# Running the query projection of a graph attention layer inside the stage before it

## The reference, cut to what matters

```python
x = _layernorm(x + _L2_gnn_ref(x, ...), axis=-1)       # third layer; its end is "L2b" and the norm "self"
...
q = linear(x, wq, bq)
k = linear(x, wk, bk)
scores = jnp.sum(q[dst] * k[src], axis=-1) * scale
...
out = jax.ops.segment_sum(v[src] * attn[:, None], dst, num_segments=n)
x = layer_norm(x + out + linear(x, ws, bs), g1, b1)
```

## Time and profile before

| what | value |
|---|---|
| median of 3 runs | 3149.26 us (3144.26 to 3154.49) |
| profiled execution: its span, which is also all that the page gives of its own time | 3626.7 us |
| busy in the profile: PE, PEld | 2379.2 us (66%), 1641.7 us (45%) |
| busy: DVE, ACT, POOL | 1987.0 us (55%), 1393.1 us (38%), 2230.6 us (62%) |
| chain that ended last: PE, issue, DVE, unknown | 39%, 21%, 15%, 14% |
| mean granted TensorE clock | 0.711 |

### The profile page before, as it was taken

The page is one execution under the profiler, slowest core; times in us unless marked ns, Lnnn a source line. Parts: engine busy times, 40 slices in busy tenths (PEclk is TensorE's granted clock), DMA queues, the critical chain, the costliest instruction groups (busy, mean ns, idle before and its releaser), DMA issues.

```text
span 3626.7 us, 45558 instructions
## 1 busy us (share of the span) xinstructions
PE 2379.2 (66%) x9551; PEld 1641.7 (45%) x9551; DVE 1987.0 (55%) x7379; ACT 1393.1 (38%) x3670; POOL 2230.6 (62%) x2460
## 2 busy tenths in 40 slices
PE   5655556838777774667777624554556588888888
PEld 2323334724444442344444424444454356555567
DVE  4554446536666673566666813333345366666677
ACT  2444544413333343333333513333343244444444
POOL 5666663566676657666766356666644366666636
PEclk7677677955666677666666755555555789999999
DMA  6656654234444423344444122222212255555411
GB/s 198 176 173 169 172 173 135 63 107 113 114 115 115 114 68 101 108 114 114 116 115 113 26 44 45 47 47 45 47 36 74 74 154 154 155 155 154 148 53 49
DMA packets 247934, 389.14 MB, mean 107 GB/s; under 512 B 58944, under 2 KB 161366, under 8 KB 247673
## 3 DMA queue, kind: packets, MB, share of 16 engines
q0 software_dynamic: 92032, 230.64, 24.6%
q1 hardware_dynamic: 155641, 155.59, 14.0%
HBM read 331.11 MB, written 54.91 MB: 106 GB/s over the span
## 4 chain that ended last, share of the span: by engine, by line
PE 39%; issue 21%; DVE 15%; another core or an unknown queue 14%; POOL 4%; ACT 3%; DVEq 2%; DMA 1%; SPq 0%; POOLq 0%; ACTq 0%
PE PS L1798 20%; PE PS L1719 6%; PE PS L1690 4%; DVE ACC L1323 3%; PE PS L1852 3%; POOL work L690 2%; DVE ACC L1090 1%; DVE work L1294 1%; PE PS L1776 1%; POOL rstd L579 1%; DVEq L376 1%; PE PS L1835 1%; PE PS L1748 1%; PE PS L1769 1%
## 5 line engine op out<-in xcount | busy, mean ns | idle before, releaser
L690 POOL DMA_INDIRECT work<-t_z,srcK x1248 | 1228.2, 984 | 610.8 <-issue 302.5
L1798 PE MATMUL PS<-work,M 128*128 128x260 f32 (+3 forms) x3328 | 1303.0, 512 | 447.6 <-issue 229.0
L1798 PEld LDWEIGHTS PS<-work,M 128*128 128x128 f32 x3328 | 757.4, 270 | 672.1 <-issue 480.2
L1323 DVE TENSOR_TENSOR ACC<-ACC,PS 128x260 f32 (+3 forms) x1614 | 588.7, 365 | 212.7 <-PE PS L1798 117.6
L2026 ACT ACTIVATE M<-iota,dloc 128x128 f32<-128x128 f32 x1248 | 396.9, 389 | 665.3 <-PE PS L1798 308.4
L690 POOL DMA_INDIRECT work<-t_x,srcK x416 | 394.0, 947 | 269.5 <-PE PS L1798 142.2
L690 POOL DMA_INDIRECT work<-in_x,srcTile x392 | 374.8, 956 | 212.2 <-issue 103.7
L1690 PE MATMUL PS<-work,M 128*128 x832 | 313.0, 519 | 240.8 <-issue 120.0
L1690 PEld LDWEIGHTS PS<-work,M 128*128 128x128 f32 x832 | 187.5, 250 | 361.5 <-issue 338.6
L1294 DVE TENSOR_TENSOR work<-work 128x256 f32<-128x256 f32 x800 | 329.1, 412 | 22.4 <-issue 14.2
L1719 PE MATMUL PS<-Y,w 128*128 x832 | 282.3, 425 | 72.2 <-issue 34.8
(11 more groups left out here) (266 smaller groups left out, 2928.9 us busy)
## 6 DMA issues: line engine op xcount, KB each, us to landing
work<-t_dhot SPq DMA_DIRECT2D x416, 128.0 KB
t_hot<-M SPq DMA_DIRECT2D x104, 256.0 KB
M<-t_hot SPq DMA_DIRECT2D x104, 256.0 KB
work<-t_z,srcK POOLq DMA_INDIRECT x1248
t_dhot<-work SPq DMA_DIRECT2D x104, 128.0 KB
work<-t_edge SPq DMA_DIRECT2D x104, 64.0 KB
work<-t_x,srcK POOLq DMA_INDIRECT x416
t_z<-Y SPq DMA_DIRECT2D x50, 130.0 KB, 2.0
```

The costliest lines, as they stand in the source:

```text
L690: pool.indirect_dma_start(out=slots[:, j, 0:width], out_offset=None, in_=table[:, :], in_offset=bass.IndirectOffsetOnAxis(ap=sources[:, k: ...
L1323: ins = vec.tensor_tensor(sums, sums, PS[k % SUMS[stage]][:, 0:cols], ALU.add)
L1798: mm(PS[k % n][:, 0:cols], M[:, k % (4 * G), :], slots_of[:, k % RING[stage], 0:cols], start=True, stop=True)\
```

## The change

The stage Q is dissolved. On PE, ACT and DVE a new helper `beside` takes one slot of the second part of L2b's dense stage and then one slot of the query work, and at the end finishes what is left of the queries. The lags of the query work are 2 (turn), 4 (product), 3 (copy) and 7 (put). It has semaphores of its own (`kept_turned`, `kept_copied`). POOL and SP are untouched. PE waits for the last sum of the pass before the second part, since the queries use the four banks of the sums. The clearing of `ACC` now stands behind all of `put_query`.

```diff
+def beside(main, other):
+    for _ in main:
+        next(other, None)
+    finish(other)
...
-        TURNS = ["L0", "L1", "L2a", "L2b", "Q", "T", "L3"]
+        TURNS = ["L0", "L1", "L2a", "L2b", "T", "L3"]
...
+        kept_turned = signal("kept_turned", {"Q": BLOCKS})
+        kept_copied = signal("kept_copied", {"Q": BLOCKS})
...
-            def gat_edges(stage, hops):
+            def gat_edges(stage, hops, other=()):
...
-                if stage == "L3":
-                    flow([(0, put_query)])
...
-                    finish(slots(EARLY, BLOCKS, hops))
+                    beside(slots(EARLY, BLOCKS, hops), iter(other))
...
-                              (7, free_variance("self", kept, "L2b")), (6, mean_variance("self"))])
+                              (7, free_variance("self", kept, "L2b")), (6, mean_variance("self"))],
+                      slots(0, BLOCKS, [(7, put_query)]))
...
-            def gat_edges(stage, hops, behind=0):
+            def gat_edges(stage, hops, behind=0, other=()):
...
-                    finish(slots(EARLY, BLOCKS, hops))
+                    if other:
+                        pe.wait_ge(sum_added.sem, sum_added.at(stage, STEPS))
+                    beside(slots(EARLY, BLOCKS, hops), iter(other))
...
-            gat_edges("L2b", [(0, turned_block("L2b", ACC, loop_added, 1, HID)), (2, self_branch)], 4)
-            flow([(0, turned_block("Q", X, kept)), (1, queries)])
+            gat_edges("L2b", [(0, turned_block("L2b", ACC, loop_added, 1, HID)), (2, self_branch)], 4,
+                      slots(0, BLOCKS, [(2, turned_block("Q", X, kept, signal=kept_turned, copied=kept_copied)), (4, queries)]))
...
-            finish(slots(EARLY, BLOCKS, outs))
-            flow([(0, turned_copy("Q", xT))])
+            beside(slots(EARLY, BLOCKS, outs), slots(0, BLOCKS, [(3, turned_copy("Q", xT))]))
```

More of the change, by code:

```diff
@@ L1841, in turned_input, with turned_block @@
                 return turned(layer, lambda b, v: rows[:, INPUT + v, 0:D], input_ready, in_turned, in_copied, 0, chunks)
-            def turned_block(layer, tile, ready, chunks=KC, width=D):
-                return turned(layer, lambda b, v: at_block(tile, b)[:, 0:width], ready, in_turned, in_copied, None, chunks)
+            def turned_block(layer, tile, ready, chunks=KC, width=D, signal=in_turned, copied=in_copied):
+                return turned(layer, lambda b, v: at_block(tile, b)[:, 0:width], ready, signal, copied, None, chunks)
             def turned_middle(layer):
@@ L1927, in queries @@
             def queries(b, v, r):
-                pe.wait_ge(in_copied.sem, in_copied.at("Q", b + 1))
+                pe.wait_ge(kept_copied.sem, kept_copied.at("Q", b + 1))
                 if due(b - 1):
@@ L2097, in work @@
                 def work(b, v, r):
-                    act.wait_ge(in_turned.sem, in_turned.at(layer, b + 1))
+                    act.wait_ge(kept_turned.sem, kept_turned.at(layer, b + 1))
                     if due(b - 1):
@@ L2101, in work @@
                     sc.activation(o[:, b % 2, :, :], turn_bank(layer, b)[:, 0:D].rearrange("p (k n) -> p k n", k=KC), ACT.Copy)\
-                        .then_inc(in_copied.sem, 1)
+                        .then_inc(kept_copied.sem, 1)
                 return work
```

## The result

| | median of the runs | ratio to before |
|---|---|---|
| before | 3149.08 us (3140.82 to 3154.50, 20 runs) | |
| changed | 3157.05 us (3149.41 to 3160.39, 20 runs) | 1.0023, 95% interval 1.0017 to 1.0029 |

The kernel became slower by 5 to 9 us, which is within the 0.3% that was called no change. The profiled execution of the changed kernel is an ordinary one: its span is 3147.5 us and its own time 3149.41. The forecast of 3593 us for the profiled execution failed, because what had lengthened the profiled execution of before by 477 us did not come back. So a new profile of the unchanged kernel is needed as the other side of the comparison.

What follows compares the result with a forecast made beforehand. The prediction took POOL's stream of gathers to bound the kernel. Start 2, middle 0, drain 2 and tail 3 delay L3's gathers by 7 us; less 1 for gather 48 gives +6 us, 3155 us, range 3128 to 3170.

Steps and rivals of the forecast that it cites:

- start: DVE's slot 7 of L2b's second part ends with put 0, which waits for PE's product 0: +2.0 us.
- middle: DVE's 2.17 us slots: a put of 0.43 us fits into the 0.65 us wait for POOL: 0 us.
- drain: DVE's slots where blocks only leave have no wait, so six puts cost at most 2.6 us; taken as +2.0.
- tail: End of the dense stage: puts between DVE's last shifts +1.0, ACT's last applied behind a query copy +2.0; together +3.0 us.
- gather 48: L3's gather that waits for the first summed step; the change saves its wait, 0 to 3 us, taken as -1.
- Stage Q is already hidden, by a hair: Before L3: step 0 would release gather 48 at 2842.2, and by its own pace it is due at 2842.3.
- PE at 2.4 GHz from about 2757: Mixed slots: PE works without a gap from slot 2, so its slot takes 1.65 us, faster than DVE's 2.17.
- rival B: PE stays at 1.2 GHz in the mixed part: last block 28 us late, 3177 us; chance 0.17 with partial forms.
- In the runs about 3 us are left for all waits of all gathers together: All passes: 2056 gathers at 1.252 us plus 571.7 us give 3146.5 us; the runs need 3149.26.
- A: The profiled 50.89 us wait in L3 exists in the runs: 34 us back, 3115 us; chance 0.19 with partial forms.
- C: L3 is bound by PE, not by gathers, so the earlier first summed step counts: -7 us, 3142; chance 0.12.
- D: The queries aren't ready when L3 could start, so it starts as before; needs PE at 1.2 GHz; no chance given.

Runs made afterwards that it cites:

- e0: The kernel before, unchanged, run and profiled a second time: 3143.37 us, ratio 1.0005 to before.
- e3: The changed kernel with the lag of put_query 8 in place of 7, so that put 0 doesn't wait: 3145.70 us, ratio 1.0013 to before.
- e4: The changed kernel with query work only in the first 15 slots of DVE and 14 of PE and ACT, the rest afterwards: 3149.94 us, ratio 1.0009.
- e7: The changed kernel with query work in the first slots only and POOL's scale_outs ahead of all power: 3148.07 us, ratio 1.0005 to before.
- e6: The changed kernel with POOL's 15 scale_outs ahead of all power: 3151.56 us, ratio 1.0011 to before.
- e1: The kernel before with the query projection left out altogether: 3143.31 us, ratio 1.0008 to before.
- e2: The kernel before with each of the 25 query products made twice: 3160.19 us, ratio 1.0059 to before.
- e5: The kernel before with POOL's 15 scale_outs ahead of all power: 3141.12 us, ratio 0.9976 to before.

## Why the prediction was right

Its mechanism and its sum held, the sum with some luck at the start. Counted in the two ordinary profiles, e0 and the changed kernel:

| step | predicted us | measured us | from |
|---|---|---|---|
| start: put 0 waits for product 0 | +2.0 | +2.1 | slot 8 of DVE against e0's, both from the last gather |
| middle: puts in the wait for POOL | 0 | 0 | 2.17 us a slot before and after, slots 8 to 13 |
| drain: six puts | +2.0 | +1.8 | (1.54 - 1.25) x 6 |
| tail, last `shift` | +1.0 | +1.0 | the remainder up to the last `shift`: 0.7 in the tail, 0.3 in slot 14 |
| tail, ACT's last `applied` | +2.0 | +2.0 | behind the copy at 2454.86 |
| start of L3's gathers | +7 | +6.85 | 82.51 - 75.66 |
| gather 48 | -1 (0 to -3) | 0 | 0.30 us before it in e0 and after |

The rows show where the delay arises in these two profiles; e3 shows that a term need not come back in full when its wait is taken away. The 0.3 us of slot 14 belong to the middle, which the prediction put at nothing. The dense stage alone explains 6.85 us of the 5 to 9 us; the 1 us of gain that was taken off for gather 48 isn't there. The sum could be read from a disturbed profile because the rows that it used were not disturbed: DVE's slots take 2.17 and 1.25 us in e0 too. Of the single steps:

- *Start, +2.0:* right in size, with luck. It rests on product 0 at 1.2 GHz. Product 0 took 1.93, 1.92, 1.46, 1.13 and 1.08 us in the profiles of the changed kernel, e4, e7, e6 and e3, and each 0.1 us less is 0.1 us less of put 0's wait (2.31, 2.31, 1.85 and 1.52 us; e3 has no such wait). With the product of e6 the start would have been +1.3. The turn of `X` was put at 0.3 us and takes 0.43 (2791.01 to 2791.44 in the profile of before), which changes little.
- *Stage Q is already hidden, by a hair:* right. The first dot was put at 37.3 us after the first gather and came at 36.09; the slack was put at 0.1 us and is 1.3. e1 shows that the stage was free, e2 that the next 19.9 us were not.
- *PE at 2.4 GHz from about 2757:* right. 2757 was 1.0 us ahead of DVE's slot 9. In e0 slot 9 begins at 2429.22, 51.5 us after the last gather of L2b, so the forecast stands for 50.5 us after it; the rise came with the product at 2428.00, 52.2 us after it, 1.7 us later than forecast. This was also the point that decided rival B, whose 28 us are not there: PE's slot at 2.4 GHz is 2429.64 - 2428.00 = 1.64 us, below DVE's 2.17.
- *Slack after the change:* put at 14 us. Sum 0 starts at 2501.07, gather 48 would be free at 2501.94 and is due at 2518.40: 16.5 us. The change bought 15 us of cover that nothing uses, and the start of the gathers came 6.85 us later for it.
- *"In the runs about 3 us are left for all waits of all gathers together":* wrong in its working, though what it concluded for gather 48 was right. It set a pace of 1.252 us for all passes beside 571.7 us of other time "unchanged". In e0 the five streams take 2618.6 us, and not 2574.8, and the rest 3142.0 - 2618.6 = 523.4, and not 571.7. Two errors of 44 and 48 us cancelled. The gathers of L1 are slower by themselves (POOL is busy 416.37 us with it against 392.12 in L2b), and the stages between the passes were also lengthened in that profile, 84.00 us against 75.66. The agreement within 3 us was a coincidence, and a reader should not trust such a sum until the disputed wait has been looked at in a second profile.
- *The first gather about 7 us later than the 84 us of before:* wrong as a reading of that profile. In it the stretch from gather to gather is 84.5 us, and in the changed kernel 82.51, less and not more. The 7 us appear only against the 75.66 of e0.
- *The profiled execution at 3593 us:* wrong, 3147.5. It assumed that every profile would be disturbed as that of before. The nine taken since have spans of 3135.7 to 3158.1 us.

The rivals: A (the profiled wait is real, 3115 us) falls with e0 and e1. The prediction set the 477 us against the Trainium skill, "Runtime: NRT & Kernel Launch", section on the preamble/postamble breakdown, where a profile's total lies about 6.2 us above the runtime's execution time. But 477 us is the distance between a profiled execution and the median of others. Within one execution the span lies 1.8 us below its own time in e0 and 1.9 in the changed kernel. Whether these are the two quantities that the page compares, no run here shows. B (PE stays at 1.2 GHz) falls with the window of 1.00. C (L3 bound by PE, -7 us) falls with e1, in which sum 0 comes 15 us earlier at no gain. D (queries late) falls with the last put at 2462, ahead of the clearing.

What stays open: what held up the first profiled execution; why the last store took 0.4 us longer in e4 and e7; why L3's gathers took 520.9 to 521.4 us in e4, e5 and e7 and 519.8 to 520.2 in the others that had no wait; and what put 0's wait costs alone.

## What to carry to other kernels

A stage that stands in the trace with a long wait behind it may cost nothing; ask what its end releases and when that is due by its own pace. Work that was hidden behind a stream of gathers need not be free when it is moved ahead of the gathers' start. Here it was free in the slots where DVE waited for POOL anyway, and cost 6.85 us at the start, in the draining slots and in the tail of the same stage, all of them on the path to the last stored block. An experiment that moves one wait can make another, as e3 did: look in its trace for the new one before its gain is read. Where a profile is longer than the runs by more than a per cent, take another one before a number of it is used.

## What the runs showed of the hardware that was not expected

One profiled execution out of ten was 15% longer, with stalls of 10 us and more whose releaser the profile doesn't see, while the first 48 gathers of L3 kept their pace of 1.252 us. The undisturbed pace of a gather on POOL is 0.95 us for the instruction and 0.30 us before the next, and holds over all of L3 (415 intervals in 519.8 to 521.4 us in eight profiles), whether the ring's slots have long been free (the changed kernel) or only just (e0). And more work made PE faster: with L2b's own products alone it was busy 49.43 of the 75.66 us of the stage and kept a clock of 0.50, with the queries among them it worked almost without a gap (5.67 of 6.00 us before 2426) and had 1.00 from its second query product on, 3.1 us after the first. The moment of the rise differs between executions of the same work: product 0 began 49.1 to 49.2 us after the last gather of L2b in five profiles and took 1.08 to 1.93 us. At 1.2 GHz the added work would have set the pace of the stage: PE's slot with product 0 takes 2426.66 - 2423.44 = 3.22 us, above DVE's 2.17.
